# Gated delta rule and FFN on one core: x loaded into the tile of the gated products' high halves, transfers issued in parts, and new instruction lists

## The reference

```python
x_act = tanh(x);  static_out = x_act @ W.T             # q = k = heads of x_act, v = heads of static_out
S = lam * S                                            # per head, one token after another
u = beta * (v_t - S.T @ k_t);  S = S + outer(k_t, u);  o_t = S.T @ q_t
y = layernorm(static_out + o) * gamma + beta_ln
x1 = layernorm(x + y)
ffn = (silu(x1 @ wg.T) * (x1 @ wu.T)) @ wd.T           # 768 hidden, int weights / 127
out = layernorm(x1 + ffn)
```

## Time and profile before

| | us |
|---|---|
| median of 3 runs | 1710.55 |
| the runs | 1705.41, 1710.55, 1717.15 |
| the profiled execution | 1699.24 |
| its span in the trace | 1697.4 |
| TensorE busy | 1362.5 (80%) |
| VectorE busy | 1352.3 (80%) |
| ScalarE busy | 1115.9 (66%) |
| GpSimd busy | 842.8 (50%) |

### The profile page before, as it was taken

The page is one execution under the profiler, slowest core; times in us unless marked ns, Lnnn a source line. Parts: engine busy times, 40 slices in busy tenths (PEclk is TensorE's granted clock), DMA queues, the critical chain, the costliest instruction groups (busy, mean ns, idle before and its releaser), DMA issues.

```text
span 1697.4 us, 53741 instructions
## 1 busy us (share of the span) xinstructions
PE 1362.5 (80%) x21032; PEld 1062.5 (63%) x21032; DVE 1352.3 (80%) x3461; ACT 1115.9 (66%) x2357; POOL 842.8 (50%) x1106
## 2 busy tenths in 40 slices
PE   4357888888888888888888888887888888888764
PEld 3345676666666666666666666666666666666542
DVE  5588888888888888888888888888788788888841
ACT  3335777667767776676777677766667677676544
POOL 6124455555544655454455555445555544555542
PEclk9557889989989998898899899898999899899877
DMA  4556445565655555566455566654565555455200
GB/s 121 118 109 119 106 122 121 119 124 114 130 118 120 122 122 116 114 123 130 110 120 119 120 125 117 125 116 115 115 116 121 114 131 117 118 117 120 52 23 25
DMA packets 701325, 190.98 MB, mean 113 GB/s; under 512 B 620944, under 2 KB 688528, under 8 KB 701072
## 3 DMA queue, kind: packets, MB, share of 16 engines
q1 hardware_dynamic: 701072, 187.56, 52.1%
HBM read 103.55 MB, written 67.11 MB: 101 GB/s over the span
## 4 chain that ended last, share of the span: by engine, by line
DVE 29%; SPq 18%; PE 16%; DMA 13%; issue 12%; ACT 8%; POOL 4%; ACTq 0%; POOLq 0%; DVEq 0%
SPq L1059 8%; DMA xa<-L_attn_x 6%; PE pc L182 6%; DMA scr_g<-gs 5%; PE pg L253 4%; DVE tt L451 4%; SPq L1072 4%; PE pu L253 4%; DVE gs L443 3%; DVE gate L495 3%; SPq L994 3%; DVE xt L406 2%; DVE x1lo L488 2%; DVE U L382 2%; DVE R L377 2%
## 5 line engine op out<-in xcount | busy, mean ns | idle before, releaser
L953 POOL TENSOR_TENSOR hlo<-gate,hhi 128x512 f16<-128x512 f32 x192 | 264.0, 1385 | 357.0 <-ACT hhi L783 354.9
L182 PE MATMUL pc<-R,tb 128*128 128x32 f16 x4096 | 158.1, 186 | 119.3 <-DVE R L372 117.3
L182 PEld LDWEIGHTS pc<-R,tb 128*128 128x128 f16 x4096 | 146.7, 118 | 139.8 <-DVE R L372 137.7
L182 PE MATMUL pc<-U,kb 128*128 128x32 f16 x4096 | 158.9, 188 | 85.3 <-DVE U L382 85.1
L182 PEld LDWEIGHTS pc<-U,kb 128*128 128x128 f16 x4096 | 146.9, 118 | 114.7 <-DVE U L382 114.6
L182 PEld LDWEIGHTS pc<-S,e 128*128 128x128 f16 x4096 | 150.1, 118 | 67.9 <-DVE S L399 64.4
L182 PE MATMUL pc<-S,e 128*128 128x32 f16 x4096 | 157.1, 186 | 41.5 <-DVE S L399 41.4
L279 PE MATMUL pd<-wd_t,hhi 128*128 128x256 f16 x768 | 174.5, 274 | 7.5 <-POOL hlo L953 5.1
L279 PE MATMUL pd<-wd_t,hlo 128*128 128x256 f16 x768 | 174.1, 274 | 0.0
L216 PEld LDWEIGHTS pf<-xb,e 128*128 128x128 f16 x4096 | 153.8, 118 | 31.5 <-DMA e<-scr_x 16.3
L216 PE MATMUL pf<-xb,e 128*128 128x32 f16 x4096 | 156.3, 191 | 17.5 <-DMA e<-scr_x 15.9
(11 more groups left out here) (132 smaller groups left out, 3222.4 us busy)
## 6 DMA issues: line engine op xcount, KB each, us to landing
xa<-L_attn_x SPq DMA_DIRECT2D x128, 128.0 KB
scr_x<-xt SPq DMA_DIRECT2D x64, 256.0 KB, 2.1
xb<-scr_x SPq DMA_DIRECT2D x256, 64.0 KB, 2.9
e<-scr_x SPq DMA_DIRECT2D x256, 64.0 KB, 3.7
scr_g<-gs SPq DMA_DIRECT2D x32, 512.0 KB, 3.5
gh<-scr_g SPq DMA_DIRECT2D x32, 512.0 KB, 3.3
kb<-k SPq DMA_DIRECT2D x512, 32.0 KB, 2.3
scr_t<-t SPq DMA_DIRECT2D x64, 256.0 KB, 3.6
```

Of the source, the lines that this page charges most:

```text
L182: last = pe.matmul(pc2[:, :, cols], stationary(h, a), moving[:, :, cols], start=a == 0, stop=a == 1)
L953: pool.tensor_tensor(hlo[:, t, :], gate[:, t % 2, :], hhi[:, t, :], ALU.subtract).then_inc(SEM["hl"], 1)
```

## The change

(a) `xs` is a view of the first four of the six tiles of `hhi`, with the bytes of a sweep's x. The first sweep's x still goes into `xa`; every later one goes into `xs`, and the tanh reads there and writes `xa`. So the load of x of sweep q now waits for the down products of sweep q - 4, which read `hhi` last, and for the tanh of sweep q - 1, which read `xs`; the tanh waits for `nr` of q - 1. `act_multiply` of sweep q - 3, which writes `hhi` again, stands behind the tanh of q on ScalarE. (b) The loops of 8 or 4 transfers take a range, so that a group of them can be issued in two to four parts with others in between. Number and size of the transfers are as before. (c) The step functions of all five engines are written in another order; the operations are the same. FIRST, LAST become -6, NS + 1, and s is counted otherwise in each list.

```diff
+        xs = hhi[:, 0:4, :].rearrange("p t n -> p (t n)").bitcast(F32).rearrange("p (n d) -> p n d", n=NW)
-        FIRST, LAST = -3, NS + 3
+        FIRST, LAST = -6, NS + 1
         def act_activate(act, q, p):
             act.wait_ge(SEM["xin"], n_of("xin", q))
-            act.activation(xa[:, :, :], xa[:, :, :], ACT.Tanh).then_inc(SEM["xa"], 1)
+            act.wait_ge(SEM["nr"], n_of("nr", q - 1))
+            act.activation(xa[:, :, :], (xs if q else xa)[:, :, :], ACT.Tanh).then_inc(SEM["xa"], 1)
-        def sp_load_x(sp, q, p):
-            sp.wait_ge(SEM["xtp"], n_of("xtp", q - 1))
-            sp.sem_inc(s_hop, 1)
-            sp.wait_ge(SEM["nr"], n_of("nr", q - 1))
+        def sp_load_x(sp, q, p, chunks):
+            if q == 1 and chunks[0] == 0:
+                sp.wait_ge(s_ps, NJ)
+                sp.sem_inc(s_hop, 1)
+            if chunks[0] == 0:
+                sp.wait_ge(SEM["dn"], n_of("dn", q - 4))
+                sp.sem_inc(s_hop, 1)
+                sp.wait_ge(SEM["xa"], n_of("xa", q - 1))
+            for n in chunks:
+                sp.dma_start(xs[:, n, :], x[:, q * T + n * C:q * T + (n + 1) * C, :]).then_inc(SEM["xin"], 16)
-        def sp_load_residual(sp, q, p):
+        def sp_load_residual(sp, q, p, chunks):
...
+            if chunks[0] == 0:
+                sp.wait_ge(SEM["x1"], n_of("x1", q - 1))
+            for n in chunks:
         def sp_step(sp, s, p):
...
+            if live(s + 3):
+                sp_load_residual(sp, s + 3, 1 - p, range(0, 2))
+                sp_load_residual(sp, s + 3, 1 - p, range(2, 4))
```

More of the change, by code:

```diff
@@ new lines, in pe_step @@
+            if live(s + 1):
+                pe_down(pe, s + 1, 1 - p, 0, range(4, 6))
+            if live(s + 4):
+                pe_gram(pe, s + 4, p, 2, range(0, 8))
+                pe_gram(pe, s + 4, p, 2, range(8, 16))
+                pe_gram(pe, s + 4, p, 3, range(0, 8))
+            if live(s + 3):
+                pe_keys_by_update(pe, s + 3, 1 - p, 0)
+            if live(s + 4):
+                pe_gram(pe, s + 4, p, 3, range(8, 16))
+            if live(s + 1):
+                pe_down(pe, s + 1, 1 - p, 1, range(0, 3))
+                pe_down(pe, s + 1, 1 - p, 1, range(3, 6))
@@ new lines, in pe_step @@
+            if live(s + 3):
+                pe_inverse_by_rest(pe, s + 3, 1 - p, 2)
+            if live(s + 4):
+                pe_static_out(pe, s + 4, p, 3)
+            if live(s + 3):
+                pe_keys_by_update(pe, s + 3, 1 - p, 2)
+            if later(s + 5):
+                pe_transpose_keys(pe, s + 5, 1 - p, 0)
+                pe_transpose_keys(pe, s + 5, 1 - p, 1)
+            if live(s + 3):
+                pe_keys_by_state(pe, s + 3, 1 - p, 3)
+                pe_inverse_by_rest(pe, s + 3, 1 - p, 3)
@@ new lines, in dve_step @@
+            if live(s + 2):
+                dve_gram(dve, s + 2, p, 2)
+            if live(s + 1):
+                dve_state_high(dve, s + 1, 1 - p, 0)
+            if live(s):
+                dve_attention_norm(dve, s, p, 2)
+            if live(s + 1):
+                dve_state_sum(dve, s + 1, 1 - p, 0)
+            if live(s + 2):
+                dve_gram(dve, s + 2, p, 3)
+            if live(s + 1):
+                dve_state_low(dve, s + 1, 1 - p, 0)
+            if live(s + 2):
+                dve_scale_keys(dve, s + 2, p, 1)
@@ new lines, in dve_step @@
+            if live(s + 2):
+                dve_invert_scale(dve, s + 2, p, 5)
+                dve_invert_add(dve, s + 2, p, 5)
+            if live(s + 1):
+                dve_state_high(dve, s + 1, 1 - p, 2)
+                dve_state_sum(dve, s + 1, 1 - p, 2)
+                dve_state_low(dve, s + 1, 1 - p, 2)
+            if later(s + 3):
+                dve_transpose_keys(dve, s + 3, 1 - p, 0)
+            if live(s + 2):
+                dve_invert_scale(dve, s + 2, p, 6)
+            if later(s + 3):
+                dve_transpose_keys(dve, s + 3, 1 - p, 1)
@@ new lines, in sp_step @@
+            if live(s + 4):
+                sp_store_gram(sp, s + 4, p)
+            if live(s + 3):
+                sp_load_inverse(sp, s + 3, 1 - p, 1, range(0, 2))
+                sp_load_inverse(sp, s + 3, 1 - p, 1, range(2, 4))
+                sp_load_inverse(sp, s + 3, 1 - p, 1, range(4, 6))
+                sp_load_inverse(sp, s + 3, 1 - p, 1, range(6, 8))
+            if live(s + 4):
+                sp_load_gram(sp, s + 4, p)
+            if later(s + 5):
+                sp_load_x(sp, s + 5, 1 - p, range(0, 2))
@@ new lines, in sp_step @@
+            if live(s + 1):
+                sp_store_out(sp, s + 1, 1 - p, range(0, 1))
+                sp_store_out(sp, s + 1, 1 - p, range(1, 2))
+            if later(s + 5):
+                sp_load_x(sp, s + 5, 1 - p, range(2, 4))
+            if live(s + 1):
+                sp_store_out(sp, s + 1, 1 - p, range(2, 3))
+            if live(s + 4):
+                sp_load_kb(sp, s + 4, p, 0, range(0, 2))
+                sp_load_kb(sp, s + 4, p, 0, range(2, 4))
+                sp_load_kb(sp, s + 4, p, 0, range(4, 6))
@@ new lines, in sp_step @@
+            if live(s + 1):
+                sp_store_out(sp, s + 1, 1 - p, range(3, 4))
+            if live(s + 4):
+                sp_load_kb(sp, s + 4, p, 0, range(6, 8))
+            if later(s + 5):
+                sp_store_keys(sp, s + 5, 1 - p, 0)
+                sp_store_keys(sp, s + 5, 1 - p, 1)
+            if live(s + 3):
+                sp_load_residual(sp, s + 3, 1 - p, range(0, 2))
+                sp_load_residual(sp, s + 3, 1 - p, range(2, 4))
+            if later(s + 5):
+                sp_spread_keys(sp, s + 5, 1 - p, range(0, 2))
+                sp_spread_keys(sp, s + 5, 1 - p, range(2, 4))
+                sp_spread_packed_keys(sp, s + 5, 1 - p, range(0, 2))
+                sp_spread_packed_keys(sp, s + 5, 1 - p, range(2, 4))
+                sp_spread_keys(sp, s + 5, 1 - p, range(4, 6))
@@ L1164, in _ @@
             sp_store_keys(eng, 0, 0, 1)
[L1165 to L1166 removed]
+            sp_spread_packed_keys(eng, 0, 0, range(B))
+            sp_spread_keys(eng, 0, 0, range(B))
             all_steps(eng, sp_step)
```

694 lines of the change are left out of this document (318 added, 376 removed).

## The result

| | before | changed |
|---|---|---|
| median, us | 1709.13 (4 runs, 1705.41 to 1717.15) | 1734.68 (4 runs, 1734.12 to 1743.31) |
| profiled execution, us | 1699.24 | 1734.42 |
| its span, us | 1697.4 | 1732.6 |

The ratio is 1.0153, with a 95% interval of 1.0112 to 1.0195: slower by 1.5%. The forecast was 1706 us, no change; its range, 1678 to 1740, reached this far for the sake of the second rival.

The account below looks back on a forecast made before the run. No engine is full, so waits bound the kernel. Terms -0.6 + 0.65 + 0.15 - 0.3 = -0.1 us a period over 28 periods, -3 us from the median 1710.55: 1707.5, rounded to 1706, called the same; range 1678 to 1740.

Parts of the forecast that it names:

- second rival: SP's key spreads wait behind the residual's load, making the gram late; 1 us more a period, 1740; chance 0.22.
- The keys through SP: Key spreads on SP stand behind the residual's load and its wait for x1; +28 us at 1 us a period; chance 0.22.
- the parts: Transfers issued in parts: as many and as large as before, same issue time, so nothing in the sum.
- The wait for x, -0.6: ScalarE's tanh no longer waits for x's load, once x has its own tile; -0.6 us a period, bounds -0.61 and 0.
- the sign: ScalarE's waits should show no tanh row for DMA, or one under 0.1 us a period.
- The chain part, +0.65: Recurrence from window 1's keys-by-state product to next gate0: new lists add 0.65 us a period, bounds 0 and 1.3.
- Window 1, -0.2: ScalarE's square moves behind the update copy, no longer ahead of the residual's copy; -0.2 us a period.
- Window 2, +0.4: ScalarE's gram copy, ahead of R's copy, waits for VectorE's mask, and inverse steps hold the update; +0.4 us a period.
- Rest, +0.45: Window 3: more inverse halves on VectorE between the state's and R's low halves; +0.45 us a period.
- The dense part, +0.15: From gate0 to window 1's keys-by-state product: VectorE waits for silu and scale-keys; +0.15 us mean, bounds -0.2 and +1.0.
- The clock, -0.3: Later static-out products recover half of the half-clock cost behind gate0; -0.3 us a period, bounds -0.6 and +1.4.
- The first: Rival: slack in the chain's hops hides the new order's cost; -0.9 to -1.2 us a period, 1680; chance 0.30.

Follow-up runs that it names:

- e3: The kernel before with x loaded into xs and that load moved ahead of the load of the inverse's second half on SP: 1691.37 us, ratio 0.9876.
- i1: The changed kernel with only one of the residual's four transfers in every sweep but the first, for timing alone: 1714.64 us, ratio 1.0031.
- g4: e3 with the residual's load moved ahead of the key spreads on SP, in one piece: 1746.69 us, ratio 1.0232.
- e4: SP's whole new list and the new tile, under the old lists of the four other engines: 1769.7 us, ratio 1.0344.
- e1: The changed kernel with SP's residual loads behind the first ten key spreads instead of ahead of them: 1752.67 us, ratio 1.0229.
- f1: The changed kernel with the residual's loads behind the first ten key spreads and VectorE's residual add behind the sixth multiplication: 1726.33 us, ratio 1.0067.
- g1: f1 with the last six key spreads also issued ahead of the residual's load and the inverse's store: 1794.29 us, ratio 1.0507.
- h1: The changed kernel with the residual's loads issued by GpSimd instead of SP: 1964.13 us, ratio 1.1481.
- i2: e3 with only one of the residual's four transfers in every sweep but the first, for timing alone: 1689.51 us, ratio 0.9878.
- e2: The kernel before with x loaded into xs, the load staying at SP's old place: 1712.96 us, ratio 0.9991.
- h3: e3 with ScalarE's square and VectorE's square sums behind window 1's update: 1701.1 us, ratio 0.9942.
- f4: f1 with VectorE's statistics of window 0 behind window 1's update instead of ahead of it: 1726.89 us, ratio 1.0079.
- g2: e3 with ScalarE's copy of the gram ahead of its copy of R in window 2: 1702.01 us, ratio 0.9974.
- g3: e3 with VectorE's new list of window 3, inverse steps 6 to 10 pulled ahead of x1lo: 1707.5 us, ratio 0.9987.
- f2: f1 with VectorE's old list in window 3: 1749.72 us, ratio 1.0209.
- j1: The changed kernel with window 0's R sum and low half ahead of the fifth multiplication on VectorE: 1739.12 us, ratio 1.0167.

## Why the forecast was wrong, step by step

**The keys through SP: the step that failed.** The prediction put this at 0.22, at one more microsecond a period, and left it out of the sum. It is the largest single part of the loss that a run isolates, 18 to 20 of the 43 us between e3 and the change (i1). In the sum the term "the parts" stood at nothing, because "their issue time is the same"; measured are 24.8 us of waits for the gram and `tb`, 0.9 a period. The rival's arithmetic nearly held: it had the last landing at x1 + 15.4, measured is 15.8 on the mean (15.0 to 17.5 over the 28 periods), and the mean gram product of the change starts at x1 + 15.9 (x1 stands 3.44 us before gate0 on the mean, the gram 12.49 behind it). Its own comparison had the gram late in a period at full clock, and set against it that the spreads often take 1.4 less. They seldom do: by SP's timelines the sixteen take 9.1 us on the mean before, in 5 of 27 periods 8.3 or less, and 9.9 in the change. It is not the parts that cost this, for g4 issues them whole and takes 9.9, and i1 has them in parts and takes 9.0. What the slow ones share is four residual loads ahead of the spreads or among them (e4 10.0, e1 10.5, f1 10.6 too); without these it is 9.0 to 9.2 (e3, g1, h1 too). Why spreads take longer behind these loads is open. Three comparisons carry the cause: e3 to g4 (only the residual's place, +55 us), the change to i1 (only the number of loads ahead, -20 us, with i2 as its control), and the change to f1 (-8 us). The second wait, that for `tb`, the prediction did not have: SP's list is one line, and the inverse's store and loads stand behind the same spreads. "Their issue time is the same" was right of the parts and wrong of the list.

**The wait for x, -0.6.** Right in size: 17.1 us became 4.1.

```profile
ACT xa L677 <- DMA hhi<-L_attn_x: 4.1, 9, 0.8
```

That is 0.15 us a period, above the 0.1 that I had set as the sign. But the prediction read `xa` as what holds the load, and e2 shows that SP's place does. Nor does the change load x earlier: SP issues it from 29.7 to 34.4 us after gate0, before from 29.6 to 32.3. The wait shrank because the tanh now starts at 38.9 instead of 36.3, near the 38.6 that the replay gave. e3 gets the whole gain by one move of the load.

**The chain part, +0.65.** It grew by 0.49, from 25.14 to 25.63. That net figure contains the gain from x, about 0.5 to 0.6 of it in window 2 (9.06 before, 8.49 in e3). So the new lists cost about 1.0 against e3 (25.63 to 24.66), where the prediction had 0.65:
- Window 1, -0.2: it was +0.14, and h3 shows the move of the square as +0.15 in this window in e3's lists. The waits that are new there are for GpSimd, which the replay left out, ScalarE's first (28 periods) and VectorE's second (27 periods):

```profile
ACT v L749 <- POOL nq L927: 44.7, 28, 1.8
```

```profile
DVE st L470 <- POOL v L919: 35.3, 27, 1.3
```

  Before, ScalarE waited there too, 34.0 us for another result of GpSimd (`nm`). f4 moves the second one behind the update and gains nothing, so VectorE's wait has no price.

- Window 2, +0.4: 8.49 in e3, 8.81 in the change, +0.3. About right, and g2 agrees with +0.2 in the window.
- Rest, +0.45: 7.53 to 8.13, +0.60, and alone in e3's lists +1.2. The mechanism (more inverse halves ahead of R) was right, the size too small.

**The dense part, +0.15.** It grew by 0.83, though the clock gave some 0.36 back: 1.2 to explain. The waits for gram and `tb` are 24.8 / 28 = 0.9 of it. The rest I put down to the new order: VectorE's waits for silu and scale-keys, which the prediction expected, are there,

```profile
DVE gate L495 <- ACT gate L777: 34.0, 84, 1.9
DVE k L412 <- ACT k L699: 32.5, 47, 1.9
```

against 26.7 and 2.8 us before. The silu itself, on ScalarE, now waits for GpSimd's low halves, which read the same `gate` tile; before there was no such wait:

```profile
ACT gate L777 <- POOL hlo L952: 43.1, 48, 1.9
```

Which part of these reaches TensorE no run isolates; i1 shows that GpSimd's low halves are what TensorE waits for next.

**The clock, -0.3.** About right. The way from gate0 to window 0's product holds seven products before and eight after, each 0.87 us at 2.4 GHz: 6.05 and 6.92 us. Measured are 6.59 and 7.10 on the mean, so the half clock (1.2 GHz) costs 0.54 and 0.18: -0.36. The granted clock over the steady part stayed at 0.91, below the 0.92 to 0.94 that I gave for this term. Where else it is lost is open; the waits for transfers alone are not the reason, for i1 has none and shows 0.90.

**The first and the third rival.** The first (the order costs nothing, 1680) fell with g2, g3 and h3; even e3, which has x's gain and none of the new lists, stays 11 us above its time. The third (the clock goes the other way) did not happen: the slow start shrank to 0.18 us.

**The ledger.** x early -21 (e3), the keys' place on SP +18 to +20 (i1 less i2's share), window 3's list +16 (g3), gram copy +11 (g2): +24 to +26 us, where the medians differ by 25.5. This agreement is luck. h3's +10 is left out of it. The prices come from medians of different chips; by the ratios, each to the kernel before on its own chip, g3 is 19 us, g2 17, i1's gain 21 and the sum some 35. And they were taken in two different sets of lists: the residual ahead costs 55 us in e3's and 18 to 20 in the change's. Prices of an order do not simply add, as f2 shows too.

## To carry to other kernels

When a list of one in-order queue is changed, write down for every transfer behind a moved one when its reader needs it, and treat a comparison that comes out at "just late" as a loss on the mean, not as a tie. A wait inside such a queue costs all that stands behind it; moving single transfers (e1, f1, g1) handed most of the lateness on or made it worse. Before a whole order is replaced, try the one move that carries the gain: here a new tile and one load that goes ahead of another gave 1.2%, and the rest of the new order took it away twice over.

## What the hardware showed that I had not expected

**VectorE held by GpSimd.** Window 0's low half of R on VectorE in the change, then GpSimd at the same time:

```profile
1226.31 0.47 DVE L366 SCALAR_TENSOR_TENSOR Sp<-pc,dcol,R 128x256 f32<-128x256 f32 x1
1226.82 1.33 DVE L372 SCALAR_TENSOR_TENSOR R<-Sp,R 128x256 f16<-128x256 f32 x1
```

```profile
1226.54 0.20 POOL L943 TENSOR_TENSOR nm<-nm,rs 128x4 f32<-128x4 f32 x1
1226.69 2.49 POOL L952 TENSOR_TENSOR hlo<-gate,hhi 128x512 f16<-128x512 f32 x2
```

The same instruction takes 0.42 us where no hlo product runs, and 1.28 on the mean here, in 27 of 28 periods with such a product beside it. In j1, some 0.7 us earlier from x1lo, it takes 0.43:

```profile
1229.81 0.43 DVE L372 SCALAR_TENSOR_TENSOR R<-Sp,R 128x256 f16<-128x256 f32 x1 [0.41 <-ACT R L658]
```

Operations that read one input from PSUM are not stretched: R<-pc,dcol,v takes 0.47 us in 28 overlaps with an hlo product and 0.48 otherwise, gate<-pu,gate 0.69 in 55 and 0.68. By the Trainium skill, SBUF — State Buffer (SBUF: two separate sides), a VectorE instruction with two SBUF inputs and a GpSimd instruction that reads SBUF take a shared pair of ports in turn, each for a whole instruction. The trace agrees here: both inputs of R<-Sp,R are in SBUF, and it ends about when the first of the two products does. In j1 and in window 1, though, it overlaps a small GpSimd row by 0.3 to 0.4 us and still takes 0.43, so not every overlap is seen to stretch it; why is open.

**Transfers issued by GpSimd.** SP issues the residual's four loads in 2.67 us. In h1 GpSimd issues them like this, by its timeline:

```profile
905.88 0.67 POOL L1097 DMA_DIRECT2D res<-L_attn_x  x1 [4.47 <-ACT xr L757]
910.89 0.59 POOL L1097 DMA_DIRECT2D res<-L_attn_x  x1 [4.34 <-issue]
914.61 0.59 POOL L1097 DMA_DIRECT2D res<-L_attn_x  x1 [3.12 <-issue]
917.94 0.59 POOL L1097 DMA_DIRECT2D res<-L_attn_x  x1 [2.75 <-issue]
```

and by its waits:

```profile
POOL res L1097 <- issue: 253.7, 75, 4.3
```

253.7 us in 75 times (25 periods): 3.4 us ahead of each further transfer, about 4 us with its own row, against 0.67 on SP. GpSimd then comes late with everything else, and the kernel is 15% slower. By the Trainium skill, DMA: Bandwidth & Descriptors (SWDGE vs HWDGE vs iDMA), a transfer of GpSimd has its descriptors written by software into SBUF, and VectorE can lock it out in its 2-port modes. The trace speaks against such a lock as the main part of the 3.4 us: 28 of the pauses in h1's timeline, among them the last one above (2.75 us), fall where VectorE does nothing at all, and they still last 2.70 us on the mean.
